# A third PSUM bank for the scores of two cross-attentions, and two in place of three for maxima and transposes

## The reference

```
# layer 0: 8 key/value heads, each serves 4 query heads; low-rank additions to all weights
q, k, v = hidden@Wq + 2*(hidden@Aq@Bq), traces@Wk + ..., traces@Wv + ...
scores = einsum('bhqd,bhtd->bhqt', q, k) / sqrt(HD)
attn   = softmax(scores, axis=-1)
out    = hidden + lora_linear(einsum('bhqt,bhtd->bhqd', attn, v), Wo, Ao, Bo)
# layer 1: 32 key/value heads, biases, a mask on the keys, then a layer norm
x      = hidden + (softmax(where(mask, Q@K.T/sqrt(HD), -inf)) @ V) @ Wo.T + bo
result = (x - mean) / sqrt(var + 1e-05) * ln_g + ln_b
```

## Time and profile before

| | us |
|---|---|
| median of 3 runs (1935.24 to 1938.48) | 1937.78 |
| the profiled execution | 1935.51 |
| its span, first to last instruction | 1933.7 |
| TensorE busy | 1825.2 (94%) |
| VectorE busy | 1268.2 (66%) |
| ScalarE busy | 1027.6 (53%) |
| GpSimd busy | 186.0 (10%) |

### The profile page before, as it was taken

The page is one execution under the profiler, slowest core; times in us unless marked ns, Lnnn a source line. Parts: engine busy times, 40 slices in busy tenths (PEclk is TensorE's granted clock), DMA queues, the critical chain, the costliest instruction groups (busy, mean ns, idle before and its releaser), DMA issues.

```text
span 1933.7 us, 43919 instructions
## 1 busy us (share of the span) xinstructions
PE 1825.2 (94%) x18340; PEld 1134.5 (59%) x18340; DVE 1268.2 (66%) x2743; ACT 1027.6 (53%) x2040; POOL 186.0 (10%) x268
## 2 busy tenths in 40 slices
PE   6899999999999999999999999999999999999985
PEld 3556455565454655555566666666667566666652
DVE  1566666666677777766665667767676767767751
ACT  0055555555555555555554555655555555655562
POOL 2010111102120001021100100001000100001001
PEclk8799999999999999999999999999999999999996
DMA  6911325212352222225422544233533236324300
GB/s 189 243 46 27 78 61 156 52 23 65 78 149 37 42 44 61 42 77 145 84 48 47 107 75 88 41 54 50 110 54 54 38 54 121 48 34 64 50 6 11
DMA packets 65030, 138.13 MB, mean 71 GB/s; under 512 B 12540, under 2 KB 49436, under 8 KB 64832
## 3 DMA queue, kind: packets, MB, share of 16 engines
q1 hardware_dynamic: 64832, 135.33, 34.5%
HBM read 97.84 MB, written 34.89 MB: 69 GB/s over the span
## 4 chain that ended last, share of the span: by engine, by line
PE 84%; ACT 6%; DVE 5%; issue 2%; DMA 2%; SPq 1%; POOL 1%; POOLq 0%
PE value L733 21%; PE work L644 12%; PE score L710 11%; PE work L627 11%; PE score L715 10%; PE ring L690 7%; ACT p_sb L799 4%; PE work L666 3%; PE work L764 3%; DVE chunk_max L904 3%; PE ring L678 2%; PE ring L743 1%; PE work L650 1%; DMA ctx_sb<-ctxT 1%; DMA k_stack<-k_dram 1%
## 5 line engine op out<-in xcount | busy, mean ns | idle before, releaser
L799 ACT ACTIVATE p_sb<-score 124x512 f32<-124x512 f32 (+1 forms) x1664 | 905.3, 597 | 746.6 <-PE score L710 391.0
L904 DVE TENSOR_REDUCE chunk_max<-ring 128x1 f32<-128x402 f32 x2048 | 1071.3, 571 | 318.1 <-PE ring L690 296.2
L690 PE MATMUL ring<-k_stack,q_stack 64*128 64x402 f32 x2048 | 766.3, 433 | 18.9 <-DVE chunk_max L904 13.5
L733 PE MATMUL value<-p_sb,v_sb 124*32 124x256 f32 x6656 | 447.4, 390 | 0.0
L690 PEld LDWEIGHTS ring<-k_stack,q_stack 64*128 64x128 f32 x2048 | 349.1, 186 | 64.9 <-DVE chunk_max L904 52.2
L715 PE MATMUL score<-q_stack,k_stack 64*124 64x256 f32 (+1 forms) x1664 | 332.2, 316 | 19.0 <-ACT p_sb L799 16.4
L710 PE MATMUL score<-q_stack,k_stack 64*124 64x512 f32 (+1 forms) x832 | 331.0, 466 | 9.9 <-ACT p_sb L799 7.9
L644 PE MATMUL work<-wv,ctx_sb 64*124 64x128 f32 x3840 | 323.2, 281 | 9.4 <-ACT v_sb L828 1.7
L644 PEld LDWEIGHTS work<-wv,ctx_sb 64*124 64x124 f32 x3840 | 284.0, 185 | 37.9 <-PE work L644 17.8
L715 PEld LDWEIGHTS score<-q_stack,k_stack 64*124 64x124 f32 (+1 forms) x1664 | 219.3, 184 | 138.7 <-ACT p_sb L799 71.6
L627 PE MATMUL work<-ctx_sb,wk 64*128 64x402 f32 x1280 | 284.9, 515 | 15.7 <-DMA ctx_sb<-ctxT 9.3
(11 more groups left out here) (68 smaller groups left out, 598.8 us busy)
## 6 DMA issues: line engine op xcount, KB each, us to landing
k_stack<-k_dram SPq DMA_DIRECT2D x288, 200.1 KB
k_dram<-k_parts SPq DMA_DIRECT2D x60, 402.0 KB, 3.0
ctx_sb<-ctxT SPq DMA_DIRECT2D x24, 992.0 KB, 6.2
k_dram<-k_parts SPq DMA_DIRECT2D x20, 395.0 KB, 2.6
q_stack<-few_rows SPq DMA_DIRECT2D x256, 2.0 KB
wq<-l_Wq SPq DMA_DIRECT2D x2, 1024.0 KB, 10.0
xt_sb<-xT SPq DMA_DIRECT2D x4, 512.0 KB, 12.3
wo<-l_Wo SPq DMA_DIRECT2D x2, 1024.0 KB, 7.0
```

What stands on the lines that cost most here:

```text
L690: engine.matmul(ring[bank_of["max", n]][:, 0:MW], q_stack[rows, u % 3, j, q * P:(q + 1) * P], k_stack[rows, 2 * (z % 3) + (u % 2 if u < L0 ...
L733: done = engine.matmul(value_bank[32 * j:32 * j + 32, 0:S], v_sb[0:tn, seq % 2, i, head * VW:head * VW + 32], p_sb[0:tn, (2 * n + j % 2) % ...
L799: engine.activation(p_sb[0:tn, n % PLACES, :], score_bank[n % 2][0:tn, :], ACT.Exp, scale=SCALE).then_inc(s_exp, 1)
L904: engine.tensor_reduce(chunk_max[:, u % 2, half, j * QT + q, c:c + 1], ring[bank_of["max", n]][:, 0:MW], AX.X, ALU.max).then_inc(s_taken[" ...
```

## The change

The number of score banks becomes a constant SCORES, 3 in place of 2, and the ring has 2 banks in place of 3; the sum stays at eight. A score n waits for the exponential n - 3. The ring's entries take the two banks in turn, so each waits for the reader of the entry two before.

```
--- before.py
+++ after.py
@@ -416,7 +416,8 @@
     EPS = 1e-5
     LEAD = 12
     PLACES = 8
-    RING = 3
+    SCORES = 3
+    RING = 2
 
     def keys_of(c):
 
@@ -505,7 +506,7 @@
         valid_rows = p_sb[0:NT, 6, 0:B * TT].rearrange("p (b t) -> p b t", b=B)
         x_rows = p_sb[32:32 + HD, 0:4, :].rearrange("p a n -> p (a n)")[:, 0:T]
 
-        score_bank = [ctx.enter_context(nc.psum_tensor(f"score{i}", [P, 512], F32)) for i in range(2)]
+        score_bank = [ctx.enter_context(nc.psum_tensor(f"score{i}", [P, 512], F32)) for i in range(SCORES)]
 
         ring = [ctx.enter_context(nc.psum_tensor(f"ring{i}", [P, 512], F32)) for i in range(RING)]
         value_bank = ctx.enter_context(nc.psum_tensor("value", [P, 512], F32))
@@ -700,19 +701,19 @@
                 elif kind == "score":
                     u, i, half = a
                     n, z, (t0, tn) = 2 * (u * NT + i) + half, stack_of(u), tile(i)
-                    if n >= 2:
-                        e.wait_ge(s_exp, n - 1)
+                    if n >= SCORES:
+                        e.wait_ge(s_exp, n - SCORES + 1)
                     stack_ready(e, z)
                     e.wait_ge(s_taken["turn q"], u + 1)
                     e.wait_ge(s_m[u % 3], 64 * (u // 3 + 1))
                     rows, slot = slice(64 * half, 64 * half + 64), 2 * (z % 3)
                     if u < L0:
-                        engine.matmul(score_bank[n % 2][0:tn, :], k_stack[rows, slot + u % 2, t0:t0 + tn],
+                        engine.matmul(score_bank[n % SCORES][0:tn, :], k_stack[rows, slot + u % 2, t0:t0 + tn],
                                       q_stack[rows, u % 3, :, :].rearrange("p j q -> p (j q)"),
                                       start=True, stop=True).then_inc(s_scores, 1)
                     else:
                         for j in range(2):
-                            done = engine.matmul(score_bank[n % 2][0:tn, j * S:(j + 1) * S],
+                            done = engine.matmul(score_bank[n % SCORES][0:tn, j * S:(j + 1) * S],
                                                  k_stack[rows, slot + j, t0:t0 + tn], q_stack[rows, u % 3, j, :],
                                                  start=True, stop=True)
                         done.then_inc(s_scores, 1)
@@ -796,7 +797,7 @@
                         e.wait_ge(s_made["turn mask"], 1)
                         for one in s_kx:
                             e.wait_ge(one, 32)
-                    engine.activation(p_sb[0:tn, n % PLACES, :], score_bank[n % 2][0:tn, :], ACT.Exp,
+                    engine.activation(p_sb[0:tn, n % PLACES, :], score_bank[n % SCORES][0:tn, :], ACT.Exp,
                                       scale=SCALE).then_inc(s_exp, 1)
                 elif kind == "read k":
                     seq, c = a
```

## The result

The changed kernel takes 2060.48 us (median of 4 runs, 2058.78 to 2061.44) against 1937.03 (4 runs, 1935.24 to 1938.48): 1.064 times as long [1.062, 1.066]. The forecast was 2079, slower, range 2022 to 2121. The span of the profiled execution went from 1933.7 to 2057.0 us, 123.3 us more, at a granted clock of 0.976 (0.973 before).

What follows compares the result with a forecast made beforehand. TensorE, issuing in program order, was taken as the bound. 62 units at 2.3 us make 143 us, two small terms cancel; added to 1935.5 this gave 2079 us, range 2022 to 2121.

Steps and rivals of the forecast that it cites:

- The scores' wait goes and the maxima's takes its place in the same 0.01 us: Between two value-matmul groups without extra maxima or transpose: nothing gained, 0.01 us lost, as ScalarE and VectorE run in step.
- One pair more, +0.49: Stretch (between two value-matmul groups) with two extra maxima: the last waits for the reduction two maxima back, 0.49 us later.
- Query transposes, +0.30: Stretch with query transposes: second maximum waits for VectorE's copy out of the bank, last maximum leaves 0.30 us later.
- Transpose of the maxima, +0.31: Stretch with the maxima's transpose: the fourth maximum waits for the transpose's reader, +0.31 us.
- Last stretch, +0.64 and +0.61: Last stretch of a unit, eight maxima: the eighth leaves later, +0.64 us in layer 0, +0.61 in layer 1.
- Output transposes and one pair more, +0.63: Stretch with output transposes and two extra maxima: second maximum waits for the transposes' last reader, last leaves 0.63 us later.
- The mis-sized step: Per unit: walked 2.38 us in a light unit, taken as 2.3 since background between second and third maximum hides a part.
- Before the first unit, +2 to +4: Before the first score, some 24 maxima one behind the other go out more slowly with two banks: +2 to +4 us.
- The end, −3: Last unit, no maxima: a score's wait for an exponential goes, about 0.5 us in each of six stretches, -3 us.
- (b): Rival: the wait only changes its owner, all stretches lose 0.01 us: 4 us in all, 1939 us; chance 3%.
- (c): Rival: slower, but mostly covered by background products: +20 to +91 us, 1956 to 2027 us; chance 9%.
- (d): Rival: the clock falls too, mean 0.9 on the 62 units, some 60 to 150 us: 2140 to 2230; chance 5%.

Runs made afterwards that it cites:

- experiment 1: Changed kernel with the third score bank taken away, leaving two score banks, two ring banks and one PSUM bank idle: 2076.39 us, 1.0761 times the kernel before.
- Experiment 3: Maxima over half of the keys, exponentials at an eighth of the scale, in both kernels: 1940.49 us with the change, 1896.2 without it.
- experiment 4: Extra pair of maxima moved behind its tile's background products, in both kernels: 2028.27 us with the change, 1922.96 without it.
- experiment 2: Kernel before, two score banks: maxima alternate between two ring banks, all transposes share the third: 2045.5 us, 1.059 times.
- experiment 5: Kernel before, third ring bank becoming a third score bank from tile 11 of the last but one unit: 1923.58 us, 0.9953 times.
- experiment 6: Kernel before with the values after every tile in place of every second: 0.9999 times the kernel before.

## Why the prediction was right, and where its size was off

The direction and the mechanism held, and the time lies in the range. The sum was 143 us and the spans differ by 123. That the sum came so near is in part luck: three kinds of stretch cost less than their terms, the end saved more than was forecast, and a term that was left out made good some of it. Step by step:

- **The scores' wait goes and the maxima's takes its place in the same 0.01 us**: shown. Plain stretches change by 0.02 us, and experiment 1 shows that the third score bank is worth 4 us in 62 units while the ring has two banks.
- **One pair more, +0.49**: the mechanism to 0.01 us (M5 0.05 behind the end of M3's reduction, 0.06 forecast), +0.43 in the unit that I had walked, 0.38 in the mean. Experiment 3 shows that it goes with the reduction, experiment 4 that background in front of the pair covers a part of it (0.26 us are left in the mean, with the new order in both kernels).
- **Query transposes, +0.30**: 0.27, in the unit and in the mean. The copy ends at 655.10 + 0.69 = 655.79 and M1 leaves at 655.85, 0.86 behind the first score; it was 0.33 in the earlier trace rows, and 0.52 later was forecast. The values follow 2.35 us after the first score, 2.08 before. VectorE and then TensorE in the changed kernel's timeline:

```profile
655.10 0.69 DVE L899 CAST q_stack<-ring 128x512 fp32r<-128x512 f32 x1 [0.89 <-PE ring L679]
```

```profile
654.99 0.49 PE L711 MATMUL score<-q_stack,k_stack 64*124 64x512 f32 x1
...
655.85 0.44 PE L691 MATMUL ring<-k_stack,q_stack 64*128 64x402 f32 x1 [0.18 <-DVE q_stack L899]
...
657.34 0.42 PE L734 MATMUL value<-p_sb,v_sb 124*32 124x256 f32 x4
```

- **Transpose of the maxima, +0.31**: M3 leaves 1.99 us after the first score, 1.68 before, as forecast, and the values +0.28 in this unit. The mean is 0.15, half. In a heavier unit of layer 1, in which the stretch takes 4.27 us, it takes 4.27 with the change as well (1316.06 to 1320.33, 1405.23 to 1409.50); that background products hide the wait there is my reading.
- **Last stretch, +0.64 and +0.61**: +0.56 in this unit, 0.40 in the mean.
- **Output transposes and one pair more, +0.63**: here the sum was too small. In the unit of the earlier trace rows M5 leaves 2.99 us after the first score, and 3.00 was the walk; the values are only 0.42 later, since M5, beside background products, had been 0.60 long and is 0.45 now: I had walked to its start and not to its end. But the mean over all units is **0.89**, and this stretch alone makes 55 of the 131 us.
- **The missing term.** The sum has nothing for the transposes of the attention output and of the next layer's input, though they take turns in the same ring. They follow those of the queries at once, and with two banks the second of them needs the bank that the queries' transposes hold. TensorE in such a unit of layer 1, changed kernel:

```profile
1454.91 0.66 PE L773 MATMUL ring<-ident,x_sb 128*128 128x128 f32 x4 [0.35 <-DVE q_stack L899]
```

The first x transpose went at 1453.96, 0.95 us earlier; in the kernel before, the second followed the first by 0.44 (1361.30 and 1361.74). The 11 units with such transposes lose 1.62 us in this stretch, the other 51 lose 0.74, so they lose some 10 us more than by the others' measure. About 4 of the 10 seem to be the clock: in three of the 11 (at 1319, 1565 and 1811 us) the stretch loses 2.5 us, in the others 1.0 to 1.5, and in the middle one of the three the granted clock was 0.67 from 1569.0 to 1574.1. The missing term is then about 6 us.
- **The mis-sized step** is the sentence "where more background lies between M1 and M2 a part is hidden by it. I take 2.3". It was right for three kinds of stretch: the pair, the transpose and the last one came out at 0.38 + 0.15 + 0.40 = 0.93 in the mean, against 1.44. In the stretch of the output it was wrong in sign, though by little once the 11 units are set apart: the other 51 lose 0.68 us in layer 0 and 0.80 in layer 1, against 0.63. A unit of layer 1 that loses 0.91 shows how, in the timeline of the changed kernel:

```profile
1420.09 0.38 PE L716 MATMUL score<-q_stack,k_stack 64*124 64x256 f32 x1
1420.10 0.44 PE L691 MATMUL ring<-k_stack,q_stack 64*128 64x402 f32 x1
1420.31 0.46 PE L716 MATMUL score<-q_stack,k_stack 64*124 64x256 f32 x3
1420.85 0.45 PE L691 MATMUL ring<-k_stack,q_stack 64*128 64x402 f32 x1
...
1421.61 0.42 PE L691 MATMUL ring<-k_stack,q_stack 64*128 64x402 f32 x1
...
1422.90 0.93 PE L691 MATMUL ring<-k_stack,q_stack 64*128 64x402 f32 x2 [0.27 <-DVE chunk_max L905]
...
1424.20 0.64 PE L734 MATMUL value<-p_sb,v_sb 124*32 124x256 f32 x8
```

The same stretch of the kernel before:

```profile
1330.53 0.44 PE L690 MATMUL ring<-k_stack,q_stack 64*128 64x402 f32 x1
...
1330.87 0.34 PE L690 MATMUL ring<-k_stack,q_stack 64*128 64x402 f32 x1
...
1331.72 0.44 PE L690 MATMUL ring<-k_stack,q_stack 64*128 64x402 f32 x1
...
1332.68 0.68 PE L690 MATMUL ring<-k_stack,q_stack 64*128 64x402 f32 x2
...
1333.72 0.64 PE L733 MATMUL value<-p_sb,v_sb 124*32 124x256 f32 x8
```

M1 leaves 0.75 us after M0 in place of 0.34, since the output's transposes hold the other bank until VectorE has read them. Twelve background products stand behind M1 and start 0.76 us after M0 in place of 0.52, and M2 behind them leaves 1.51 us after M0, 1.19 before. So its reduction is late as well, and on top of that M4 must now wait for it (0.27 on TensorE), where with three banks M4 and M5 went straight on. The two delays stand one behind the other, 4.10 us to the values in place of 3.19, +0.91. In this unit, then, the background hides nothing of a wait that comes ahead of it. Experiment 4 moves the pair, the second delay, behind the rest of the background: with the new order in both kernels this stretch loses 39.0 us in place of 55.3. In experiment 2, where transposes have a bank of their own, the same unit leaves M1 with no delay (0.33 after M0) and loses 0.49 us, which is the pair's wait alone; over the 51 units it is 0.37 there and 0.74 with the change. So about half of this stretch's loss in those units is the pair, and half the output's transposes.
- **Before the first unit, +2 to +4**: +3.0. This can't be read sharply: kernels with three ring banks and full reductions reach that point at 97.0 to 99.7 us, those whose maxima go round two at 101.3 to 105.1. **The end, −3**: −10.6, of which 7.4 are the last unit. The wait was sized about right, and the clock was missing from the sum.
- **Rivals.** (b) fell: plain stretches only. (c) is right in that a part is covered, a third of three kinds of stretch (0.93 of 1.44 us), but not most of the cost. (d) fell: the unit that took 25.52 us takes 27.44 at full clock, so in it no time went into the clock, and over the 62 units the granted clock was 0.99 in both kernels. TensorE counts as busy for 26.40 us of that unit, where I had carried over the 24.62 of before:

```profile
645.94:673.38 27.44, 26.40 (x225) 15.10 (x221) 19.36 (x41) 14.79 (x28) 2.89 (x4) 1.00 0.21 46
```

The sentence of the Trainium skill (Perfetto Trace Analysis, Optimization Strategy) that a repeated gap can mean missing room in PSUM was weighed in the prediction and left aside. Experiments 1 and 3 bear both sides out: the room pays only for the ring whose wait ends last, the one with 52.2 us of waits and not the one with 185.7. The depth-cycling that the Trainium skill describes (TensorE: Matmul & The Clock Gate, section "A second HAM failure mode: psum-queue depth-cycling") did not show as a rule in the units, at a mean granted clock of 0.99 with longer gaps than before; single falls, as that at 1569 us, stand in both traces (0.67 from 870 to 880 us before). What the last unit shows is in the last section.
- **Other signs.** VectorE's busy time was to stay at 1268 us and is 1292.0. It isn't more work: one reduction is 571 ns as before. Two reductions in a row overlap by some 0.08 us (1.06 for two of 0.57), and there are fewer such overlaps now, 905 against 1202 among the 2048 reductions. The group's time rises by 22.9 us with them (1071.3 and 1094.2).

## What to carry to other kernels

Before a buffer moves from one ring to another, write down for each ring when the wait that is removed ends and when the one that takes its place ends; if they end together the removed wait gives nothing back, and a burst of the ring that got shallower costs up to a full turn of its reader (0.49 us here, 0.38 in the mean). List every user of that ring, the rare ones too. The sum of a wait in the profile says neither: here 177 us of waits went and the kernel became 123 us slower, and an order that left the waits of the kernel before at 50 us made it 11 us faster. When the same remedy helps both kernels, compare them with the remedy in both. A step that holds a bank of the ring for a slow reader is worth looking at first, and a bank can be lent to another ring for the part of the program in which its own is idle.

## What the runs showed of the hardware

- **The clock in the last unit.** With two score banks its key tile pairs took 3.1 to 3.5 us at first and the granted clock then fell from 2.4 to 1.2 GHz, 0.67 in the mean over the unit (the earlier trace rows has one wait of 0.68 there); the pairs behind it took 4.3 to 4.5 us. With three banks, pairs of 2.6 us, it stayed at 1.00 through that unit, in the changed kernel as in experiment 5. The changed kernel's window over the last unit:

```profile
2012.70:2027.60 14.90, 12.20 (x134) 7.11 (x130) 0.98 (x4) 11.21 (x22) 0.00 (x0) 1.00 0.00 1
```

The third experiment's kernel without the change has two score banks and kept its full clock there:

```profile
1837.90:1855.60 17.70, 13.61 (x134) 7.38 (x130) 0.98 (x4) 12.13 (x23) 0.00 (x0) 1.00 0.00 1
```

So of the 7.4 us between 22.3 and 14.9, about 2.8 are the wait (17.7 to 14.9) and about 4.6 the clock. The number of banks doesn't decide it, though. Experiment 4's kernel with the change has three score banks, and its last unit ran at 1.2 GHz:

```profile
1975.90:1998.70 22.80, 21.24 (x134) 11.55 (x130) 0.99 (x4) 11.39 (x23) 0.00 (x0) 0.50 0.00 1
```

In experiment 1, with two banks, it was 0.75, and in experiment 6, with two banks, 1.00. What makes the clock fall there stays open; at the end of a program like this one a few us between two kernels can be the clock alone.

- **A matmul overtakes.** In layer 1 a score is two matmuls of 256 columns on one half of the rows, and the maximum behind them works on the other half. In the stretch above, M0 starts at 1420.10, and the score's second matmul, ahead of it in program order, at 1420.31; its first had started at 1420.09.
- **The length of a matmul depends on its neighbours.** In these profiles, whose matmul ends are modelled, a maximum of 402 columns is 0.44 to 0.45 us alone, 0.34 close behind another, and 0.65 beside background products (at 656.33 in the changed kernel, also at full clock). In a walk through a timeline the ends have to be walked as well as the starts.
